# Four graph layers on one core: the first layer's relation made row by row and turned by transposes, its norm from ScalarE's squares, its centring on GpSimd

## The chip, the cores and the metric

The kernel runs on 1 core of one Trainium2 chip. The metric is the device time of one execution in microseconds, the median of several runs. All times below are microseconds unless marked ns.

## The reference

There are 64 graphs of 128 nodes with 256 features each, and one adjacency matrix `adj` (128 x 128, zeros and ones) for all. Four layers follow each other, each of the form x = x + layer(relu(layernorm(x))). The change touches the first:

```python
def _L0_gnn_ref(neuron_states, adjacency, Wq, Wk, Wv):
    q = jnp.einsum('bnd,ed->bne', neuron_states, Wq)
    k = jnp.einsum('bnd,ed->bne', neuron_states, Wk)
    v = jnp.einsum('bnd,ed->bne', neuron_states, Wv)
    rel = jnp.einsum('bnd,bmd->bnm', q, k)
    rel = adjacency.T[None, :, :] * rel
    rel = rel / jnp.linalg.norm(rel, axis=2, keepdims=True)
    return jnp.einsum('bnm,bmd->bnd', rel, v)
...
h = jnp.maximum(_layernorm(x, axis=-1), 0.0)
x = x + _L0_gnn_ref(h, adj, L0_gnn_Wq, L0_gnn_Wk, L0_gnn_Wv)
```

The other three are an attention with a leaky ReLU, a product with the normalised adjacency, and an attention with 8 heads.

## The kernel before

All of x stays in SBUF (`xs`). The graphs are worked on in 32 pairs, and each layer goes through all pairs before the next begins. Each engine has its own instruction stream, written by hand, and semaphores tie the streams together; so the order in which a function stands in an engine's `step` is the order in which that engine does it. In the first layer `step(p)` is run for p = 1 to 30 on TensorE (PE), with what comes before pair 1 and after pair 30 written out around it.

For pair p the work of the first layer is, in the order of its data:

- VectorE (DVE) takes the mean and variance of both graphs (`statistics`, lines 115 to 130: two BN_STATS, two BN_AGGR, then `nmean` and `vare`), GpSimd (POOL) raises the variance to the power -1/2 (`inverse_root`, line 141), and DVE's `normalise` (line 526) writes the centred features `xn`.
- PE turns them by four transposes into bank `HT` (`turn`, line 152). ScalarE (ACT) makes the rounded part of their ReLU (`relu_high`, line 390), DVE the remainder (`low_part`, line 569), and ACT once more the full one, `hT` (`relu_T`, line 395). A product of rounded and remainder parts takes 3 matmuls where one of full precision stood.
- PE multiplies by the joint weight of q and k (`t_product`, 12 matmuls, line 246), and ACT copies the result (`copy_t`, line 399). PE multiplies by the weight of v (`values`, 12 matmuls, line 246); ACT makes the rounded part (`copy_v`, line 404) and DVE the remainder (`low_v`, line 581).
- PE makes the relation matrix (`relation`, line 308) in bank `RR`, with the receiving node along the free dimension, and DVE multiplies it by `adj` (`mask`, line 576, tile `relm`). ACT makes its rounded part (`relation_high`, line 409), GpSimd its remainder (`relation_low`, line 468) and its squares (`squares`, line 464).
- In `outputs(p)` PE first sums the squares over the partitions by products with a column of ones (line 316, bank `NO`), and then multiplies the relation by the values (6 matmuls, line 321, bank `OO`). DVE copies the sums (`copy_norm2`, line 586), GpSimd raises them to -1/2 (`inverse_norm`, line 473), and DVE adds the scaled result to x (`update`, line 591).

PE's `step(p)` is `t_product(p)`, `turn(p+1)`, `values(p)`, `relation(p)`, `outputs(p-1)`. There is one `hT`, one pair `hTs` of rounded part and remainder, and one `relm`; so `relu_high(p+1)` waits until `values(p)` has read `hTs`. The second layer's first product (line 236) waits for the last `update` of the first layer. During steps 1 to 6 ACT and DVE also split the later layers' weights (lines 413 and 565).

## Time and profile before

| | before |
|---|---|
| median of 3 runs | 769.87 (768.22 to 770.98) |
| the profiled execution: its time | 770.85 |
| the profiled execution: its span, first to last instruction | 769.1 |
| busy: PE, PEld, DVE, ACT, POOL | 722.0, 668.5, 648.3, 551.6, 485.8 |
| mean granted TensorE clock, share of full | 0.984 |

PE is TensorE's matmuls, PEld its weight loads, which run beside them: each matmul has one load, and a matmul on full-precision operands that are not turned shows as two or more of each. The span is that of one profiled execution, and what lies around it is the difference of the first two of its numbers. The first layer takes the stretch from the start to 191.6; the rest of the span belongs to layers that the change does not touch.

### The profile page before, as it was taken

What the parts mean: (1) busy time and instruction counts of PE and PEld (TensorE: products, weight loads), DVE (VectorE), ACT (ScalarE), POOL (GpSimd) and SP (SyncE); (2) the same over time, 40 slices, a digit from 0 to 9 for tenths busy, and PEclk for the clock granted to TensorE, in tenths of its full rate; (3) what the DMA queues carried; (4) which work ended last, traced back from release to release, by engine and by line L of the source; (5) the groups of instructions that cost most, each with busy time, mean ns of one, the idle gap of its engine ahead of it and who ended that gap; (6) DMA issues with size and microseconds to landing.
All of it is one profiled execution on the core that took longest, in us unless ns stands there. A gap on an engine that the chain in (4) does not pass through costs nothing.

```text
span 769.1 us, 23106 instructions
## 1 busy us (share of the span) xinstructions
PE 722.0 (94%) x7001; PEld 668.5 (87%) x7001; DVE 648.3 (84%) x2709; ACT 551.6 (72%) x1768; POOL 485.8 (63%) x615
## 2 busy tenths in 40 slices
PE   6999999997999989869999899999999999999995
PEld 5999999997777777769998799999999999999984
DVE  5898888887699999969998788888888888888863
ACT  3554545443578778756663899999999999999985
POOL 1445455456477877668884667666667666667652
PEclk9999999999999999979999999999999999999999
DMA  7333200000000000000000000000000000000001
GB/s 231 96 97 96 68 0 0 0 0 1 1 1 1 2 1 1 1 1 0 0 0 1 2 29 29 14 28 28 27 28 28 14 28 28 27 28 28 14 29 42
DMA packets 21681, 20.15 MB, mean 26 GB/s; under 512 B 2432, under 2 KB 21632, under 8 KB 21632
## 3 DMA queue, kind: packets, MB, share of 16 engines
q1 hardware_dynamic: 19440, 18.16, 7.4%
q10 hardware_dynamic: 2192, 1.44, 0.7%
q8 instruction: 17, 0.28, 0.1%
q14 instruction: 32, 0.26, 0.1%
HBM read 11.21 MB, written 8.39 MB: 25 GB/s over the span
## 4 chain that ended last, share of the span: by engine, by line
PE 76%; DVE 16%; issue 3%; ACT 1%; POOL 1%; DMA 1%; DVEq 0%; POOLq 0%; ACTq 0%
PE bank L246 42%; PE bank L1072 7%; PE bank L1064 5%; PE bank L1082 4%; PE bank L152 4%; PE bank L308 4%; PE bank L321 3%; PE bank L226 3%; DVE stats L115 3%; DVE xs L843 2%; DVE masked_e L819 2%; DVE leaky_e L824 2%; PE bank L236 2%; PE bank L316 2%; DVE att L837 1%
## 5 line engine op out<-in xcount | busy, mean ns | idle before, releaser
L1141 ACT ACTIVATE prob<-wide,small 128x128 f32<-128x128 f32 x512 | 199.1, 395 | 20.1 <-DVE small L1225 20.0
L1190 POOL TENSOR_TENSOR prob<-prob,small 128x512 f32<-128x512 f32 x128 | 133.1, 1040 | 106.1 <-DVE small L1239 106.1
L141 POOL TENSOR_TENSOR rstd<-vare,mhalf 128x2 f32<-128x2 f32 x128 | 88.6, 692 | 67.8 <-DVE vare L130 67.8
L1225 DVE CUSTOM_DVE_ANT_0 wide<-bank,mbias 128x128 f32<-128x128 f32 x512 | 116.0, 282 | 9.4 <-PE bank L1064 9.4
L115 DVE BATCH_NORM_STATS2 stats<-xs 128x6 f32<-128x256 f32 (+1 forms) x256 | 95.4, 414 | 5.6 <-DMA xs<-in_x_dram 4.5
L1141 ACT ACTIVATION_READ_ACCUMULATOR prob<-wide,small 128x1 f32 x512 | 98.2, 192 | 0.0
L217 POOL TENSOR_SCALAR xn<-xs,nmean,rstd 128x256 f32<-128x256 f32 x126 | 69.1, 558 | 13.6 <-POOL rstd L141 10.8
L1148 ACT COPY probT<-bank 128x512 f32<-128x512 f32 x128 | 72.0, 588 | 7.8 <-PE bank L1072 6.9
L1072 PE MATMUL bank<-ident,prob 128*128 128x128 f32 x512 | 73.8, 276 | 1.9 <-POOL prob L1190 1.7
L236 PE MATMUL bank<-w,hT 128*128 128x258 f32 x256 | 63.0, 389 | 2.3 <-DVE xs L591 1.9
L1072 PEld LDWEIGHTS bank<-ident,prob 128*128 128x128 f32 x512 | 57.1, 140 | 8.9 <-issue 6.0
L246 PE MATMUL bank<-w,yTs 128*128 128x256 f32 x384 | 55.4, 295 | 4.5 <-DVE xs L968 4.5
L152 PE MATMUL bank<-ident,xn 128*128 128x128 f32 x384 | 58.4, 275 | 0.5 <-DVE xn L1000 0.5
L236 PEld LDWEIGHTS bank<-w,hT 128*128 128x128 f32 x256 | 49.3, 194 | 10.6 <-DVE xs L591 2.2
L464 POOL TENSOR_TENSOR relsq<-relm 128x256 f32<-128x256 f32 x32 | 21.6, 676 | 56.0 <-PE bank L321 56.0
L246 PE MATMUL bank<-wo,oTs 128*128 128x256 f32 x384 | 54.8, 293 | 2.2 <-DVE oTs L1248 2.2
L246 PE MATMUL bank<-hTs,wq 128*128 128x256 f32 x384 | 55.0, 293 | 1.8 <-DVE hTs L1243 1.8
L246 PEld LDWEIGHTS bank<-w,yTs 128*128 128x128 f32 x384 | 49.5, 196 | 6.4 <-DVE yTs L963 4.7
L246 PE MATMUL bank<-wv0T,hTs 128*128 128x256 f32 x384 | 54.0, 289 | 0.7 <-DVE oTs L581 0.7
L246 PEld LDWEIGHTS bank<-wo,oTs 128*128 128x128 f32 x384 | 48.1, 192 | 6.3 <-DVE oTs L1248 2.7
L246 PE MATMUL bank<-wv,hTs 128*128 128x256 f32 x384 | 53.0, 287 | 0.0
L246 PE MATMUL bank<-hTs,m_qk 128*128 128x256 f32 x384 | 50.9, 281 | 0.8 <-DVE hTs L569 0.8
(128 smaller groups left out, 1843.8 us busy)
## 6 DMA issues: line engine op xcount, KB each, us to landing
out_dram<-xs SPq DMA_DIRECT2D x32, 256.0 KB, 2.1
xs<-in_x_dram SPq DMA_DIRECT2D x29, 256.0 KB, 2.6
xs<-in_x_dram ACTq DMA_DIRECT2D x1, 512.0 KB, 7.3
xs<-in_x_dram ACTq DMA_DIRECT2D x1, 256.0 KB, 3.8
wq<-in_L_gnn_Wq_dram SPq DMA_DIRECT2D x1, 256.0 KB, 3.4
wk<-in_L_gnn_Wk_dram ACTq DMA_DIRECT2D x1, 256.0 KB, 4.7
wv<-in_L_gnn_Wv_dram SPq DMA_DIRECT2D x1, 256.0 KB, 5.3
w<-in_L_gnn_W_dram SPq DMA_DIRECT2D x1, 256.0 KB, 7.1
```

The lines of the kernel that those rows point to most:

```text
L115: ins = nc.vector.bn_stats(stats[:, b, g, :], x_of(p, g))
L141: nc.gpsimd.tensor_tensor(rstd[:, b, :], vare[:, b, :], mhalf[:, :], ALU.pow).then_inc(rstd_ready, 1)
L152: ins = nc.tensor.transpose(pe_ps[:, c * 2 * N + g * N:c * 2 * N + (g + 1) * N], src[:, g, c * 128:(c + 1) * 128], ident[:, :])
L217: ins = nc.gpsimd.tensor_scalar(xnb[b][:, g, :], xs[:, 2 * p + g, :], nmean[:, b, g:g + 1], rstd[:, b, g:g + 1], ALU.add, ALU.mult)
L236: ins = nc.tensor.matmul(ps_g, hT[:, c, g, :], weight[:, c, :], start=(c == 0), stop=(c == C - 1))
L246: ins = nc.tensor.matmul(ps, lhsT(a, c), rhs(b, c), start=(n == 0), stop=(n == len(terms) - 1))
L1064: ins = nc.tensor.matmul(SS[r][:, (g * C + c) * N:(g * C + c + 1) * N], qT[rows_r, c, g, :], kT[rows_r, c, g, :], start=True, stop=True)
L1072: ins = nc.tensor.transpose(PT[r % 2][:, i * N:(i + 1) * N], prob[:, r, i, :], ident[:, :])
L1141: ins = nc.scalar.activation(prob[:, r, i, :], wide[:, r, i, :], ACT.Exp, bias=nmax[r][:, i:i + 1], scale=-1.0, accum_out=rsum[r][:, i:i + 1])
L1148: nc.scalar.copy(probT[:, r, :, :].rearrange("p i n -> p (i n)"), PT[r % 2][:, :]).then_inc(pt_ready, 1)
L1190: nc.gpsimd.tensor_tensor(prob[:, r, :, :], prob[:, r, :, :], rinv[r].unsqueeze(2).to_broadcast([128, QUAD, N]), ALU.mult).then_inc(prob_r ...
L1225: nc.vector.tensor_tensor_reduce(out=wide[:, r, i, :], in0=SS[r][:, i * N:(i + 1) * N], in1=mbias[:, :], scale=-1.0, scalar=3e38, op0=ALU. ...
```

## The change

Six things change in the first layer.

1. `relation` swaps its operands, so the relation has the receiving node along the partitions; `mask` multiplies it by a transposed adjacency `adjT`, made once at the start by one PE transpose and one DVE copy, and writes to one of two `relm`. PE turns the masked relation by two transposes into bank `RT` (`turn_relation`), and `relation_high` and `relation_low` read `RT`.
2. The squares and their sums are made by two ACT instructions, one for each graph, which square a row and sum it (`squares`); PE's product with ones, `copy_norm2` and the bank `NO` are gone.
3. `relation_low` moves from GpSimd to DVE, where it reads PSUM.
4. Centring moves from DVE to GpSimd (`centre`, two instructions for a pair), but for the first two pairs.
5. `hT` gets a second buffer `hT2`, and `hTs` a second one in `yTs[0]`, which the third layer uses later; so `relu_high(p+1)` no longer waits for `values(p)`.
6. The order of each engine's step is written anew, the work on the masked relation of pair p-1 now being done in step p, and `update` stands ahead of `low_v`.

```diff
+        hTs_of = [hTs, yTs[0]]
+        hT_of = [hT, hT2]
...
-                ins = nc.gpsimd.tensor_scalar(xnb[b][:, g, :], xs[:, 2 * p + g, :], nmean[:, b, g:g + 1],
+                ins = nc.gpsimd.tensor_scalar(xnb[b][:, g, :], x_of(p, g), nmean[:, b, g:g + 1],
...
+                def turn_relation(p, b):
+                    pe.wait_ge(relm_ready, p + 1)
+                    pe.wait_ge(relm_low, since(p))
+                    for g in range(2):
+                        ins = nc.tensor.transpose(RT[:, g * N:(g + 1) * N], relm[b][:, g, :], ident[:, :])
+                    ins.then_inc(rt_done, 1)
...
+                def relation(p, b):
                     pe.wait_ge(tT_ready, p + 1)
                     pe.wait_ge(hT_ready, p + 1)
                     pe.wait_ge(relm_ready, since(p))
                     for g in range(2):
                         for c in range(C):
-                            ins = nc.tensor.matmul(RR[:, g * N:(g + 1) * N], hT[:, c, g, :], tT[:, c, g, :],
+                            ins = nc.tensor.matmul(RR[:, g * N:(g + 1) * N], tT[:, c, g, :], hT_of[b][:, c, g, :],
                                                    start=(c == 0), stop=(c == C - 1))
                     ins.then_inc(rel_done, 1)
 
                 def outputs(p):
-                    pe.wait_ge(relsq_ready, p + 1)
                     pe.wait_ge(x_done, since(p))
-                    for g in range(2):
-                        nc.tensor.matmul(NO[:, g:g + 1], relsq[:, g, :], ones[:, 0:1], start=True, stop=True)
...
+                def step(p, b):
+                    t_product(p, b)
+                    turn(p + 1, 1 - b)
+                    turn_relation(p - 1, 1 - b)
+                    values(p, b)
+                    relation(p, b)
                     outputs(p - 1)
...
-                def relu_high(p):
+                def relu_high(p, b):
                     act.wait_ge(tr_done, p + 1)
-                    act.wait_ge(v_done, since(p))
-                    nc.scalar.activation(hT_high, HT[:, :], ACT.Relu).then_inc(high_ready, 1)
-
-                def relu_T(p):
+                    act.wait_ge(v_done, since(p - 1))
+                    nc.scalar.activation(flat(hTs_of[b][0]), HT[:, :], ACT.Relu).then_inc(high_ready, 1)
+
+                def relu_T(p, b):
                     act.wait_ge(low_ready, p + 1)
-                    act.wait_ge(rel_done, since(p))
-                    nc.scalar.activation(hT_flat, HT[:, :], ACT.Relu).then_inc(hT_ready, 1)
+                    act.wait_ge(rel_done, since(p - 1))
+                    nc.scalar.activation(flat(hT_of[b]), HT[:, :], ACT.Relu).then_inc(hT_ready, 1)
...
                 def relation_high(p):
+                    act.wait_ge(rt_done, p + 1)
+                    act.wait_ge(out_done, since(p))
+                    nc.scalar.copy(rels[0][:, :, :], RT[:, 0:2 * N].rearrange("p (g n) -> p g n", g=2)).then_inc(relm_high, 1)
+
+                def squares(p, b):
                     act.wait_ge(relm_ready, p + 1)
-                    act.wait_ge(out_done, since(p))
-                    nc.scalar.copy(rels[0][:, :, :], relm[:, :, :]).then_inc(relm_high, 1)
+                    act.wait_ge(rn_ready, since(p))
+                    for g in range(2):
+                        ins = nc.scalar.activation(relsq[:, g, :], relm[b][:, g, :], ACT.Square, accum_out=norm2[:, g:g + 1])
+                    ins.then_inc(n2_ready, 1)
...
+
+                def step(p, b):
                     copy_t(p)
-                    relu_high(p + 1)
-                    relu_T(p + 1)
+                    relu_high(p + 1, 1 - b)
+                    relation_high(p - 1)
+                    squares(p - 1, 1 - b)
+                    relu_T(p + 1, 1 - b)
                     copy_v(p)
-                    relation_high(p)
...
-                def squares(p):
-                    pool.wait_ge(relm_ready, p + 1)
-                    pool.wait_ge(out_done, since(p))
-                    nc.gpsimd.tensor_tensor(relsq[:, :, :], relm[:, :, :], relm[:, :, :], ALU.mult).then_inc(relsq_ready, 1)
-
-                def relation_low(p):
-                    pool.wait_ge(relm_high, p + 1)
-                    nc.gpsimd.tensor_tensor(rels[1][:, :, :], relm[:, :, :], rels[0][:, :, :].bitcast(F32),
-                                            ALU.subtract).then_inc(relm_low, 1)
-
                 def inverse_norm(p):
                     pool.wait_ge(n2_ready, p + 1)
+                    pool.wait_ge(x_done, since(p))
                     nc.gpsimd.tensor_tensor(rnorm[:, :], norm2[:, :], mhalf[:, :], ALU.pow).then_inc(rn_ready, 1)
...
+                pool.wait_ge(tr_done, 1)
+                centre(pool, 2, 0, rstd_ready, xn_ready)
+
+                def step(p, b):
+                    inverse_root(pool, p + 2, stats_ready, rstd_ready, b)
                     inverse_norm(p - 1)
-                    relation_low(p)
-                    inverse_root(pool, p + 3, stats_ready, rstd_ready)
-
-                with pool.Fori(0, PAIRS // 2 - 2) as j:
-                    step(2 * j + 1)
-                    step(2 * j + 2)
-                for n, p in enumerate(range(PAIRS - 3, PAIRS)):
-                    squares(p)
-                    inverse_norm(p - 1)
-                    relation_low(p)
-                    if n > 0:
-                        inverse_root(pool, n - 1, l1_stats_ready, l1_rstd_ready, (n - 1) % 2)
-                        if n == 1:
-                            pool.wait_ge(tr_done, PAIRS)
-                        centre(pool, n - 1, (n - 1) % 2, l1_rstd_ready, l1_xn_ready)
+                    pool.wait_ge(tr_done, p + 1)
+                    centre(pool, p + 2, b, rstd_ready, xn_ready)
+
+                for p in range(1, PAIRS - 2):
+                    step(p, p % 2)
...
+                def mask(p, b):
                     dve.wait_ge(rel_done, p + 1)
-                    dve.wait_ge(relsq_ready, since(p))
-                    dve.wait_ge(relm_low, since(p))
-                    nc.vector.tensor_tensor(relm[:, :, :], RR[:, 0:2 * N].rearrange("p (g n) -> p g n", g=2),
-                                            adj_pair, ALU.mult).then_inc(relm_ready, 1)
+                    dve.wait_ge(rt_done, since(p - 1))
+                    dve.wait_ge(n2_ready, since(p - 1))
+                    nc.vector.tensor_tensor(relm[b][:, :, :], RR[:, 0:2 * N].rearrange("p (g n) -> p g n", g=2),
+                                            adjT_pair, ALU.mult).then_inc(relm_ready, 1)
+
+                def relation_low(p):
+                    dve.wait_ge(relm_high, p + 1)
+                    nc.vector.tensor_tensor(rels[1][:, :, :], RT[:, 0:2 * N].rearrange("p (g n) -> p g n", g=2),
+                                            rels[0][:, :, :].bitcast(F32), ALU.subtract).then_inc(relm_low, 1)
 
...
-                def copy_norm2(p):
-                    dve.wait_ge(out_done, p + 1)
-                    nc.vector.tensor_copy(norm2[:, :], NO[:, 0:2]).then_inc(n2_ready, 1)
-
                 def update(p):
                     dve.wait_ge(rn_ready, p + 1)
+                    dve.wait_ge(out_done, p + 1)
...
-                def step(p):
-                    low_part(p + 1)
-                    mask(p)
-                    normalise(p + 2)
+                def step(p, b):
+                    low_part(p + 1, 1 - b)
+                    relation_low(p - 1)
+                    dve.wait_ge(xn_ready, p + 2)
+                    statistics(p + 3, 1 - b)
+                    mask(p, b)
+                    update(p - 1)
                     low_v(p)
-                    copy_norm2(p - 1)
-                    statistics(p + 3)
-                    update(p - 1)
```

TensorE's stream, a whole step before (`t_product`, `turn`, `values`, `relation`, the sums, the outputs; bank is PSUM):

```order
L246 MATMUL bank<-hTs,m_qk 128x256 x12
L152 MATMUL bank<-ident,xn 128x128 x4
L246 MATMUL bank<-wv0T,hTs 128x256 x12
L308 MATMUL bank<-tT,hT 128x128 x4
L316 MATMUL bank<-ones,relsq 128x1 x2
L321 MATMUL bank<-oTs,rels 128x256 x6
```

The same step in the changed kernel:

```order
L253 MATMUL bank<-hTs,m_qk 128x256 x12
L153 MATMUL bank<-ident,xn 128x128 x4
L304 MATMUL bank<-ident,relm 128x128 x2
L253 MATMUL bank<-wv0T,hTs 128x256 x12
L323 MATMUL bank<-hT,tT 128x128 x4
L333 MATMUL bank<-oTs,rels 128x256 x6
```

The two products with `ones` (which the trace shows as four) are gone, and two transposes of `relm` stand ahead of the 12 products for the values.

VectorE's stream before, from the `update` that ends one step (with a weight's remainder behind it, in this early step) through the next one up to its statistics:

```order
L591 SCALAR_TENSOR_TENSOR xs<-bank,rnorm,xs 128x256 x2
L565 TENSOR_TENSOR wv_1<-raw,wv_0 128x512
L569 SCALAR_TENSOR_TENSOR hTs<-bank,hTs 128x512
L576 TENSOR_TENSOR relm<-bank,adj_sb 128x256
L526 TENSOR_SCALAR xn<-xs,mv,rstd 128x256 x2
L581 TENSOR_TENSOR oTs<-bank,oTs 128x512
L586 COPY norm<-bank 128x2
L115 BN_STATS stats<-xs 128x6 x2
L122 BN_AGGR mv<-stats 128x2 x2
L129 SCALAR_TENSOR_TENSOR nmean<-mv 128x2
L130 SCALAR_TENSOR_TENSOR vare<-mv 128x2
```

The same in the changed kernel, one step, from `low_part` (here into the second buffer, `yTs`) to `low_v`:

```order
L578 SCALAR_TENSOR_TENSOR yTs<-bank,yTs 128x512
L590 TENSOR_TENSOR rels<-bank,rels 128x256
L116 BN_STATS stats<-xs 128x6 x2
L123 BN_AGGR mv<-stats 128x2 x2
L130 SCALAR_TENSOR_TENSOR nmean<-mv 128x2
L131 SCALAR_TENSOR_TENSOR vare<-mv 128x2
L585 TENSOR_TENSOR relm<-bank,adjT 128x256
L602 SCALAR_TENSOR_TENSOR xs<-bank,rnorm,xs 128x256 x2
L595 TENSOR_TENSOR oTs<-bank,oTs 128x512
```

Centring (`xn`) and the copy of `norm` have left; `rels` has come; the mask stands behind the statistics; and `low_v` (`oTs`), which stood ahead of the statistics, is last, behind `update` (`xs`).

GpSimd's stream before, one step of its loop:

```order
L464 TENSOR_TENSOR relsq<-relm 128x256
L473 TENSOR_TENSOR rnorm<-norm,mhalf 128x2
L468 TENSOR_TENSOR rels<-relm,rels 128x256
L140 REGISTER_ALU
L141 TENSOR_TENSOR rstd<-vare,mhalf 128x2
```

GpSimd's stream in the changed kernel, two steps:

```order
L142 TENSOR_TENSOR rstd<-vare,mhalf 128x2
L490 TENSOR_TENSOR rnorm<-norm,mhalf 128x2
L224 TENSOR_SCALAR xn<-xs,nmean,rstd 128x256 x2
L142 TENSOR_TENSOR rstd<-vare,mhalf 128x2
L490 TENSOR_TENSOR rnorm<-norm,mhalf 128x2
L224 TENSOR_SCALAR xn<-xs,nmean,rstd 128x256 x2
```

The two large two-input operations on the relation (`relsq` and `rels`) have left, and the two centring operations have come, behind the power for the norm.

## Rows read from the trace of the kernel before

**Rows 1.** windows of the steady first layer and its end: us, then busy us of each engine, PEclk

```profile
99.89:174.76 74.87, 74.87 (x647) 74.87 (x645) 64.73 (x197) 37.41 (x71) 38.78 (x56) 1.00 0.00 0
174.76:191.60 16.84, 12.83 (x106) 12.12 (x104) 11.54 (x39) 5.81 (x12) 10.88 (x18) 0.93 0.00 1
```

**Rows 2.** timeline of one step: start us, us, engine, line, operation [idle before <-releaser]

```profile
99.89 1.48 PEld L246 LDWEIGHTS bank<-hTs,m_qk 128*128 128x128 f32 x12
...
101.31 0.46 PEld L152 LDWEIGHTS bank<-ident,xn 128*128 128x128 f32 x4
...
101.50 0.74 DVE L115 BATCH_NORM_STATS2 stats<-xs 128x6 f32 x2
101.61 0.58 ACT L399 COPY tT<-bank 128x512 f32<-128x512 f32 x1 [0.52 <-PE bank L246]
...
101.74 1.50 PEld L246 LDWEIGHTS bank<-wv0T,hTs 128*128 128x128 f32 x12
...
102.31 0.73 POOL L468 TENSOR_TENSOR rels<-relm,rels 128x256 fp32r<-128x256 f32 x1
...
102.63 0.43 DVE L129 SCALAR_TENSOR_TENSOR nmean<-mv 128x2 f32<-128x2 f32 x1
...
103.05 0.86 DVE L591 SCALAR_TENSOR_TENSOR xs<-bank,rnorm,xs 128x256 f32 x2
103.18 0.98 PEld L308 LDWEIGHTS bank<-tT,hT 128*128 128x128 f32 x8
...
103.56 0.60 ACT L390 ACTIVATE hTs<-bank 128x512 fp32r<-128x512 f32 x1 [1.36 <-PE bank L246]
104.08 0.53 PEld L316 LDWEIGHTS bank<-ones,relsq 128*128 128x128 f32 x4
104.19 0.69 DVE L569 SCALAR_TENSOR_TENSOR hTs<-bank,hTs 128x512 fp32r<-128x512 f32 x1 [0.27 <-ACT hTs L390]
...
104.52 0.78 PEld L321 LDWEIGHTS bank<-oTs,rels 128*128 128x128 f32 x6
...
104.79 0.41 DVE L576 TENSOR_TENSOR relm<-bank,adj_sb 128x256 f32<-128x256 f32 x1
...
105.23 1.48 PEld L246 LDWEIGHTS bank<-hTs,m_qk 128*128 128x128 f32 x12
```

**Rows 3.** timeline, TensorE's weight loads, start of the program

```profile
17.18 1.47 PEld L246 LDWEIGHTS bank<-hTs,m_qk 128*128 128x128 f32 x12 [0.45 <-issue]
...
19.97 1.49 PEld L246 LDWEIGHTS bank<-wv0T,hTs 128*128 128x128 f32 x12 [0.92 <-DVE oTs L581]
```

**Rows 4.** timeline, end of the first layer and first product of the second

```profile
180.11 1.48 PEld L246 LDWEIGHTS bank<-hTs,m_qk 128*128 128x128 f32 x12
...
180.43 0.16 DVE L586 COPY norm<-bank 128x2 f32<-128x2 f32 x1 [0.34 <-PE bank L321]
...
187.04 0.88 DVE L591 SCALAR_TENSOR_TENSOR xs<-bank,rnorm,xs 128x256 f32<-128x256 f32 x2
...
190.66 0.88 DVE L591 SCALAR_TENSOR_TENSOR xs<-bank,rnorm,xs 128x256 f32<-128x256 f32 x2 [0.81 <-POOL rnorm L473]
...
191.59 3.81 PE L236 MATMUL bank<-w,hT 128*128 128x258 f32 x8 [1.93 <-DVE xs L591]
```

**Rows 5.** timeline, VectorE and GpSimd, near the end of the first layer

```profile
177.43 0.16 DVE L129 SCALAR_TENSOR_TENSOR nmean<-mv 128x2 f32<-128x2 f32 x1
...
188.45 1.09 POOL L217 TENSOR_SCALAR xn<-xs,nmean,rstd 128x256 f32<-128x256 f32 x2
...
188.97 0.20 DVE L129 SCALAR_TENSOR_TENSOR nmean<-mv 128x2 f32<-128x2 f32 x1
```

**Rows 6.** the page's costliest groups: busy us, mean ns of one

```profile
L1141 ACT ACTIVATE prob<-wide,small 128x128 f32<-128x128 f32 x512 | 199.1, 395 | 20.1 <-DVE small L1225 20.0
...
L141 POOL TENSOR_TENSOR rstd<-vare,mhalf 128x2 f32<-128x2 f32 x128 | 88.6, 692 | 67.8 <-DVE vare L130 67.8
...
L217 POOL TENSOR_SCALAR xn<-xs,nmean,rstd 128x256 f32<-128x256 f32 x126 | 69.1, 558 | 13.6 <-POOL rstd L141 10.8
```

154 lines of the change are left out of this document (77 added, 77 removed).

## The prediction, on record before the changed kernel ran

> **What bounds the kernel now.** I read the stretches first. From 99.89 to 174.76 TensorE is busy 74.87 of 74.87 us, its weight loads too, at full clock, while VectorE has 64.73, ScalarE 37.41 and GpSimd 38.78 [rows 1]. That stretch holds 14 steps, so a step takes 5.348. Next the timeline of one step [rows 2]. The weight loads of each group start when the group before them has issued, so the differences of their starts are what each group costs TensorE: `t_product` 1.42 (99.89 to 101.31), four transposes 0.43, `values` 1.44, `relation` 0.90, sums of squares 0.44 (104.08 to 104.52), outputs 0.71, together 5.34. None of these rows has idle time before it. So the middle of the first layer costs TensorE's issue time, and only what leaves or enters TensorE's stream counts there, as long as the others keep pace. The exceptions are at its two ends. At the start TensorE waits 0.45 for pair 1's remainder and 0.92 for pair 0's values [rows 3]. At the end, from the start of `t_product(31)` at 180.11 to the second layer's first product at 191.59 pass 11.48 us, in which TensorE waits for `update(30)` (187.04) and `update(31)` (190.66), and both stood behind sums, copy and power [rows 4].
>
> **The change, part by part.**
>
> *TensorE, each step.* The sums leave: 0.44. Two transposes come. Four transposes take 0.43, so two take 0.215 [rows 2]; the swap in `relation` leaves its four products of the same size. The step becomes 5.34 - 0.44 + 0.215 = 5.115, a gain of 0.225. From below the two transposes can't be less than nothing (gain 0.44); from above I take what the two sum products took, 0.44 (gain 0). I take 0.215, since it is the same operation on the same shape.
>
> *Does VectorE keep pace?* I lay a step out from t = 0 at the start of `t_product(p)`. ScalarE's `copy_t` starts at 1.72 (101.61) [rows 2] and takes 0.58, `relu_high(p+1)` 0.60 behind it, so to 2.90. (The turn has issued by 1.85, and its buffer is free, so this no longer waits for `values(p)`, as it did at 103.56.) VectorE then runs `low_part` from 2.93 (start to start with the mask 0.60 [rows 2]), `relation_low` (new: 128 x 256 from PSUM with an SBUF operand, as the mask, 0.41), the statistics, the mask 0.41, `update` and `low_v`. The statistics took 1.55 (101.50 to 103.05), of which `nmean` 0.43. The same `nmean` took 0.16 at 177.43 [rows 5]; at 102.63 it ended at 103.06, just when GpSimd's `rels` of 102.31 ended (103.04) [rows 2]. GpSimd no longer does that operation, so I take 1.28. The mask then ends at 2.93 + 0.60 + 0.41 + 1.28 + 0.41 = 5.63. `update(p-1)` needs the outputs, whose end VectorE sees 0.32 behind the next `t_product` (180.43 against 180.11 [rows 4]), at 5.44; so it starts at 5.63, takes 0.86 [rows 2], and `low_v` 0.69 (the same size and form as `low_part`) ends at 7.18, which is 2.07 in the next step. `values(p+1)` wants it at 1.42 + 0.43 + 0.215 = 2.065. So with every duration counted in full the fit is exact to 0.01, with no slack; but instructions that follow each other without a wait overlap by about 0.08 (0.60 against 0.69 [rows 2]), five times in this chain, on ScalarE too, and then `update` is bound by the outputs at 5.44 and `low_v` ends about 1.85, 0.2 early. I take no wait. This is the narrowest place of the design.
>
> *The relation's way.* Two transposes end about 2.35, `relation_high` follows `relu_high` (2.90 to at most 3.50, its bound being the 128 x 512 ReLU), `relation_low` ends at 3.94, and the outputs want it at 1.42 + 0.43 + 0.215 + 1.44 + 0.90 = 4.405. No wait. The squares are 2 ScalarE instructions with sums, not in this layer before; the fourth layer's exponentials of 128 x 128 with sums take 395 ns each [rows 6], so 0.79, and I allow 0.2 for reading out the last sum: 3.50 to 4.5. ScalarE then has some 1.0 more a step, against 37.41 of 74.87 busy [rows 1]; it is hidden under TensorE. If it were not, it would cost 30 steps of it.
>
> *GpSimd.* Squares and remainder leave, two centrings come, 558 ns each [rows 6]. Its chain is the squares' end 4.5, the power 0.69 (692 ns for the same 128 x 2 form), centring 1.12, so 6.35 with a step between engines, which is 1.23 in the next step, and `turn` wants it at 1.42. With ScalarE's overlaps it is some 0.3 earlier. Hidden. The power for the norm is ready at about 5.2, before `update`.
>
> *The start.* The two waits of rows 3 go: `relu_high(1)` need not wait for `values(0)`, and VectorE no longer centres pair 2 ahead of `mask(0)` and `low_v(0)`. One transpose for `adjT` costs 0.11. Gain 0.45 + 0.92 - 0.11 = 1.26, at least 0.
>
> *The end.* From `t_product(31)` = 0: `turn_relation(30)` to 1.64; `values(31)` waits for `low_v(30)` to about 1.9; `relation` from 3.3; outputs(30) 4.2 to 4.95; `update(30)` at 5.27, since its power is long made, to 6.15; `low_v(31)` to 6.85, `relation_low(31)` to 7.25, outputs(31) from 7.3 to 8.0, seen at 8.35; `update(31)` 8.4 to 9.3, for its power too is made beside that; the second layer's product at 9.35. Before it was 11.48 [rows 4]: gain 2.1. Bounds: 0, and 3.
>
> *Sum.* 30 steps of 0.225 = 6.75, start 1.26, end 2.1: 10.1. From the profiled execution's 770.85 that is 760.7, and since that execution was 0.98 above the median, **759.8** as a median.
>
> **The port.** While GpSimd centres (188.45, two instructions, 1.09), `nmean` inside that time took 0.20, not 0.16 [rows 5]; so centring costs VectorE's two-input operations a few hundredths. The Trainium skill (Advanced Engine Details and Errata, GPSIMD Details) says more: that GpSimd shares a read and a write interface with VectorE and conflicts with VectorE instructions that have two SBUF inputs. `nmean` is one, and in the changed order it lies where GpSimd centres. The row at 102.63 agrees, the row at 188.97 hardly does; what it would cost if it held is the second rival.
>
> **The rivals.**
>
> 1. *VectorE is late after all* (chance 0.12). For it: the chain above has no slack with full durations, and `low_v` now stands last. A step would be about as long as before, 5.3 to 5.35; only the ends gain, 3.4: 766.5. Against it: VectorE loses the centring of 2 x 256 elements, the copy (0.16 [rows 4]) and 0.27 of stretched `nmean`, and gains one operation of 0.41.
> 2. *Centring holds VectorE's `nmean`* to its end: up to 1.1, and by where the two fall in my layout about 0.7. `low_v` ends at 2.55 instead of 1.85, so `values` starts 0.5 late. The long step then gives VectorE the time back, so the wait comes in every second step: 30 x 0.25 = 7.5 lost, 767.3. Against it the 0.20 above. Chance 0.06.
> 3. *Two transposes cost what the sums did*, and the change does nothing for TensorE in the steps: ends only, 766.5. Chance 0.05.
> 4. *Slower: the ring through GpSimd.* Turn, `relu_high`, `relation_high`, squares, power, centring, next turn is one ring, 0.2 to 0.5 short of a step. It decides when it grows by more than that; to end 0.3% above the median of before it must make the step 0.19 longer than 5.34, so grow by some 0.6 to 0.9, as it would if power and centring each took half as long again (0.35 + 0.55 = 0.9). At 0.9, with 0.35 of slack, a step is 5.115 + 0.55 = 5.665: 30 x 0.325 = 9.75 lost, 3.4 gained at the ends, 776.2. For it: GpSimd's durations beside new traffic are unknown; against: 558 ns is a mean over 126 [rows 6]. Chance 0.04.
>
> *The clock at the end* goes with each case. It fell to half there: 8 products took 3.81 at 191.59 behind an idle stretch of 1.93 [rows 4], and TensorE was busy 12.83 of the 16.84 us that end there, at a mean clock of 0.93 [rows 1]. In my layout the 2.1 us that go are all idle time of TensorE. If the clock stays up, half of 3.81 comes back, 1.9, giving 757.9; I give it 4 in 10, within the forecast's case.
>
> **How the numbers follow.** Forecast 0.73, split into 759.8 and 757.9; rivals 0.12, 0.06, 0.05, 0.04. A measurement of this kernel tells about 0.3% (2.3 us) from no change. The range from 756.5 to 767.5 takes in the forecast with the clock's case, up to 1.4 more if the 0.44 bound is nearer, and rivals 1 to 3 nearly whole. Faster: the forecast and rivals 1 to 3 all end under 767.56, but rivals 1 to 3 lie near it, so of their 0.23 I count 0.06 as no change: 0.90. Slower: 0.04.
>
> **What would show it.** The step, from one `t_product` to the next, at 5.10 to 5.15 (right), at 5.3 (rival 1 or 2; then `values` loads show idle time before them, released by VectorE's `oTs`), or transposes of `relm` with a group cost of 0.44 (rival 3). `nmean` at 0.16 to 0.20 (right) or 0.5 and more (rival 2). Idle time ahead of `turn`'s transposes, released by GpSimd's `xn` (rival 4). The first `t_product`s without 0.45 and 0.92 of idle time. The end, `t_product(31)` to the second layer's product, at about 9.4. ScalarE's two squares of a pair within about 1.0. The prediction is wrong if a step is over 5.2 or if the later layers, which the change leaves alone, get longer.

## The result: 755.25 us, 1.8% faster, and outside the predicted range

| | before | after |
|---|---|---|
| median | 769.99 (768.22 to 770.98), 4 runs | 755.25 (754.75 to 756.56), 4 runs |
| ratio after to before | | 0.9818, 95% interval 0.9803 to 0.9833 |
| the profiled execution: time, span | 770.85, 769.1 | 755.72, 753.8 |
| mean granted clock | 0.984 | 0.989 |

The prediction was 759.8, range 756.5 to 767.5. The direction was right, but the change brought 14.7 us and not 10.1. The median lies 1.25 us below the range.

The middle of the first layer first. These are the windows of the kernel after, from the start of one `t_product` to that of `t_product(31)`, and from there to the second layer's first product; the columns are those of [rows 1].

```profile
94.86:171.46 76.60, 76.60 (x663) 76.60 (x661) 59.30 (x176) 45.75 (x135) 36.35 (x61) 1.00 0.01 4
171.46:180.75 9.29, 6.83 (x55) 6.18 (x53) 7.20 (x25) 3.98 (x14) 4.36 (x8) 1.00 0.01 2
```

TensorE and its weight loads are still busy the whole time, as in [rows 1], and 15 steps take 76.60, so a step takes 5.107 where it took 5.348. VectorE has gone from 86% to 77% of the stretch, ScalarE from 50% to 60%. One step in the timeline (start, duration, engine, line, operation), which answers to [rows 2]:

```profile
94.86 1.48 PEld L253 LDWEIGHTS bank<-hTs,m_qk 128*128 128x128 f32 x12
...
96.17 0.68 DVE L595 TENSOR_TENSOR oTs<-bank,oTs 128x512 fp32r<-128x512 f32 x1
96.28 0.46 PEld L153 LDWEIGHTS bank<-ident,xn 128*128 128x128 f32 x4
...
96.71 0.25 PEld L304 LDWEIGHTS bank<-ident,relm 128*128 128x128 f32 x2
...
96.93 1.49 PEld L253 LDWEIGHTS bank<-wv0T,hTs 128*128 128x128 f32 x12
...
97.81 0.33 ACT L431 ACTIVATE relsq<-relm 128x128 f32<-128x128 f32 x1
...
98.31 0.21 ACT L431 ACTIVATION_READ_ACCUMULATOR relsq<-relm 128x1 f32 x1
```

The reader is to see two things. The two transposes of `relm` cost TensorE 0.22 (96.71 to 96.93), as half of four transposes did. And no weight load has idle time before it.

Where VectorE's `nmean` meets GpSimd's centring matters further down, so here are the two kinds of meeting that this kernel shows, with the two centring instructions of a pair taken singly:

```profile
58.79 0.56 POOL L224 TENSOR_SCALAR xn<-xs,nmean,rstd 128x256 f32<-128x256 f32 x1
58.96 0.39 DVE L130 SCALAR_TENSOR_TENSOR nmean<-mv 128x2 f32<-128x2 f32 x1 [0.26 <-DVE mv L123]
...
99.28 0.56 POOL L224 TENSOR_SCALAR xn<-xs,nmean,rstd 128x256 f32<-128x256 f32 x1
...
99.78 0.16 DVE L130 SCALAR_TENSOR_TENSOR nmean<-mv 128x2 f32<-128x2 f32 x1
...
99.82 0.56 POOL L224 TENSOR_SCALAR xn<-xs,nmean,rstd 128x256 f32<-128x256 f32 x1
```

At 58.96 `nmean` began 0.17 into a centring instruction, took 0.39 and ended with it at 59.35. At 99.78 it began 0.06 before the end of the first and 0.04 before the start of the second, and took 0.16. Of the 28 meetings in this profile, 27 are of the second kind.

The end of the first layer, which answers to [rows 4]:

```profile
171.46 1.48 PEld L253 LDWEIGHTS bank<-yTs,m_qk 128*128 128x128 f32 x12
...
173.38 1.49 PEld L253 LDWEIGHTS bank<-wv0T,yTs 128*128 128x128 f32 x12 [0.26 <-DVE oTs L595]
...
178.73 0.77 PEld L333 LDWEIGHTS bank<-oTs,rels 128*128 128x128 f32 x6 [1.60 <-issue]
...
179.82 0.88 DVE L602 SCALAR_TENSOR_TENSOR xs<-bank,rnorm,xs 128x256 f32<-128x256 f32 x2
...
180.75 3.07 PE L243 MATMUL bank<-w,hT 128*128 128x258 f32 x8 [1.05 <-DVE xs L602]
```

From `t_product(31)` to the second layer's first product pass 9.29 us (11.48 before). That product takes 3.07 (3.81 before, 2.01 at full clock when the kernel was run again), since part of it still ran at half clock.

Laid side by side, the two profiled executions differ by 15.3 us of span, and the table says where. Each row is the difference of two starts of TensorE's weight loads, or of a start and the end of the span.

| stretch | before | after | gained |
|---|---|---|---|
| start to `t_product(1)` | 17.18 | 17.03 | 0.15 |
| `t_product(1)` to `t_product(31)` | 162.93 | 154.43 | 8.50 |
| `t_product(31)` to the second layer's first product | 11.48 | 9.29 | 2.19 |
| second layer, from its first product to the third layer's | 138.8 | 136.3 | 2.5 |
| third layer | 85.95 | 86.7 | -0.75 |
| fourth layer | 352.8 | 350.1 | 2.7 |

The first three rows make 10.84, beside a predicted 10.1. The other 4.5 came in code that the change doesn't touch. What is different there is seen in two places. The first is the granted clock (PEclk) in windows of the kernel before, and then of the kernel after:

```profile
189.00:196.00 7.00, 5.07 (x16) 3.75 (x15) 2.42 (x11) 0.57 (x1) 3.66 (x7) 0.51 0.00 1
329.00:336.00 7.00, 5.92 (x24) 5.56 (x25) 4.66 (x13) 4.75 (x10) 3.38 (x4) 0.51 0.01 2
...
424.00:428.00 4.00, 3.32 (x15) 3.32 (x16) 2.72 (x21) 4.00 (x21) 1.96 (x3) 0.58 0.00 0
762.00:766.00 4.00, 2.93 (x12) 2.63 (x12) 0.98 (x2) 0.00 (x0) 0.00 (x0) 0.57 0.00 0
```

```profile
181.00:184.00 3.00, 3.00 (x10) 2.33 (x10) 0.87 (x6) 0.14 (x1) 1.62 (x3) 0.59 0.00 0
314.00:321.00 7.00, 4.23 (x17) 4.05 (x18) 4.41 (x14) 5.43 (x13) 2.80 (x4) 0.55 0.00 1
...
424.00:428.00 4.00, 4.00 (x59) 3.66 (x58) 2.81 (x17) 4.00 (x20) 2.36 (x3) 1.00 0.00 0
745.00:752.00 7.00, 3.22 (x48) 2.51 (x47) 1.38 (x2) 1.17 (x2) 0.00 (x0) 1.00 0.13 40
```

The clock has two levels here, 1.2 and 2.4 GHz, and 0.50 is the lower. Before fell to it in five places (a fifth is at 342 to 347), after in three (a third is at 328 to 336), and not in the fourth layer. The second is the second layer's steps. A step here is the time from one pair's first product (`w`, `hT`) to the next pair's. From the 8th on nearly all take 4.04, and those ahead of it 3.2 to 4.0, but for the first with 5.25 before and 4.61 after. Before had one of 5.07 (the 7th, 215.34 to 220.41) and one of 5.14 (the 20th), after had none. The start of the long one in the kernel before:

```profile
214.12 1.27 POOL L797 TENSOR_TENSOR xs<-xs,exp_u 128x512 f32<-128x512 f32 x1
...
214.34 1.33 DVE L824 SCALAR_TENSOR_TENSOR leaky_e<-masked_e 128x256 f32<-128x256 f32 x1
...
215.34 1.71 PEld L236 LDWEIGHTS bank<-w,hT 128*128 128x128 f32 x8
...
218.19 0.20 PEld L686 LDWEIGHTS bank<-ident,att 128*128 128x128 f32 x2 [1.13 <-DVE att L837]
...
219.28 0.43 DVE L824 SCALAR_TENSOR_TENSOR leaky_e<-masked_e 128x256 f32<-128x256 f32 x1
...
219.41 1.44 POOL L797 TENSOR_TENSOR xs<-xs,exp_u 128x512 f32<-128x512 f32 x1
...
220.41 1.72 PEld L236 LDWEIGHTS bank<-w,hT 128*128 128x128 f32 x8
```

`leaky_e` is a VectorE operation with both inputs in SBUF. It began at 214.34 inside GpSimd's add of 214.12 to 215.39, and ended at 215.67, 0.28 behind it, having taken 1.33 where it takes 0.43. One step later it began 0.13 ahead of the add, took its 0.43, and the add took 1.44 in place of 1.27. The `leaky_e` of the other long step began at 267.93, only 0.02 ahead of the add of 267.95, and took 1.57; it too ended 0.28 behind the add's end. So a `leaky_e` that begins inside the add, or as good as together with it, ends 0.28 behind the add, while one that begins 0.13 ahead of it loses nothing. The transposes of `att` then waited until 218.19. In the profiled execution of after, the order was the harmless one, here at 202.93, in every step but the last two of the layer, in which `leaky_e` took 0.68 in both kernels:

```profile
202.93 0.44 DVE L835 SCALAR_TENSOR_TENSOR leaky_e<-masked_e 128x256 f32<-128x256 f32 x1
...
203.06 1.44 POOL L808 TENSOR_TENSOR xs<-xs,exp_u 128x512 f32<-128x512 f32 x1
```

The Trainium skill (Advanced Engine Details and Errata, GPSIMD Details) says that GpSimd shares an interface with VectorE and conflicts with VectorE instructions that have two SBUF inputs. By that rule this is the place to look, and these rows agree, with 0.90 lost for one collision. So does the row at 58.96 in the first layer, where `nmean` has two SBUF inputs.

### The profile page after: what moved, and what is told of

Read it like the earlier page. It is cut to its first block, busy times and chain, and to the rows that moved or that the text cites. A ratio compares the mean times of both kernels' runs of the same rounds, so it can differ in the third digit from the quotient of the medians.

```text
span 753.8 us, 22983 instructions
## 1 busy us (share of the span) xinstructions
PE 709.9 (94%) x6938; PEld 657.7 (87%) x6938; DVE 627.1 (83%) x2650; ACT 564.8 (75%) x1896; POOL 474.5 (63%) x610
## 3 DMA queue, kind: packets, MB, share of 16 engines
q10 hardware_dynamic: 2192, 1.44, 0.7%
## 4 chain that ended last, share of the span: by engine, by line
PE 76%; DVE 16%; issue 4%; ACT 1%; POOL 1%; DMA 1%; DVEq 0%; POOLq 0%; ACTq 0%
PE bank L253 43%; PE bank L1083 7%; PE bank L1075 5%; PE bank L1093 4%; PE bank L323 4%; PE bank L153 4%; PE bank L233 3%; PE bank L333 3%; DVE stats L116 3%; DVE xs L854 2%; DVE masked_e L830 2%; DVE leaky_e L835 2%; DVE att L848 2%; DVE small L838 2%; PE bank L243 1%
## 5 line engine op out<-in xcount | busy, mean ns | idle before, releaser
L224 POOL TENSOR_SCALAR xn<-xs,nmean,rstd 128x256 f32<-128x256 f32 x186 | 102.4, 561 | 12.8 <-POOL rstd L142 10.8
L490 POOL TENSOR_TENSOR rnorm<-norm,mhalf 128x2 f32<-128x2 f32 x32 | 22.1, 691 | 79.9 <-ACT relsq L431 79.9
L253 PE MATMUL bank<-hTs,wk 128*128 128x256 f32 x384 | 51.2, 282 | 0.0
L253 PEld LDWEIGHTS bank<-hTs,wq 128*128 128x128 f32 x384 | 47.9, 189 | 2.3 <-DVE hTs L1254 2.3
```

Source lines behind the costliest of these rows:

```text
L224: ins = nc.gpsimd.tensor_scalar(xnb[b][:, g, :], x_of(p, g), nmean[:, b, g:g + 1], rstd[:, b, g:g + 1], ALU.add, ALU.mult)
L253: ins = nc.tensor.matmul(ps, lhsT(a, c), rhs(b, c), start=(n == 0), stop=(n == len(terms) - 1))
```

## The experiments

My theory was that the 4.5 us behind the first layer come from two things that code left alone can still meet: collisions of `leaky_e` with GpSimd's add, and falls of the clock. The rivals were that they are chance of one execution, so that the change is worth its 10.8 alone, or that they hang on something else that the first layer leaves behind. The theory as written also said that the collisions move when the later layers begin some tenths of a microsecond earlier or later. Beside this, the terms of the first layer were put to a test. There are twelve runs. Where no count of rounds is named, a run is one execution, set beside the kernel before on the same chip (one execution, and seven with a median of 770.14 for the last four kernels). The kernel before alone spread from 768.22 to 770.98, so differences of 1 to 2 us are read from stretches of the profiles and not from whole times.

**Both kernels again.** No edit.

> The kernel before, once more, for the stretch that the change does not touch: from the second layer's first product to the end (769.1 - 191.6 = 577.5 us in the profiled execution of before; 753.8 - 180.75 = 573.0 in that of the changed kernel, 4.5 less with the same code). Theory A (coincidences: two-input operations of VectorE and GpSimd that meet, and where TensorE's clock falls, both hanging on phases of some tenths of a us): the stretch comes out between 574 and 579, possibly again 577.5 if the phases repeat. Theory B (something lasting that the changed first layer leaves behind): 577.5 within 0.5.

> The changed kernel, once more, same stretch. Theory A: between 571 and 576, 573.0 if the phases repeat. Theory B: 573.0 within 0.5. Both: step of the first layer 5.107, end of the first layer 9.29.

Measured: 768.99 and 754.05, the kernel before beside them 770.64. Behind the second layer's first product, 574.9 and 571.1 us of span were left, 3.8 apart (the first pair 4.5). The two long steps of the second layer came back in the kernel before at the same places (4.94 and 5.18), `leaky_e` again at 1.33 in the first:

```profile
214.91 1.27 POOL L797 TENSOR_TENSOR xs<-xs,exp_u 128x512 f32<-128x512 f32 x1
...
215.13 1.33 DVE L824 SCALAR_TENSOR_TENSOR leaky_e<-masked_e 128x256 f32<-128x256 f32 x1
```

The third layer's falls of the clock came back in both kernels. The fourth layer's did not: both took 350.1. So the 2.7 us of the fourth layer were chance of one execution, and the rest was not. In return the fall at the start of the second layer, which after had shown, was absent now. So a difference of nearly the same size came back, but made of other terms: 3.1 in the second layer (2.5 in the first pair), 0.8 in the third (-0.75) and nothing in the fourth (2.7). The two stretches fit the theory's ranges (574 to 579, 571 to 576) and lie outside those of its rival. The new order had one collision in this run, in the 6th step of 5.08, with `leaky_e` at 197.38 inside the add of 197.22 and 1.40 long. And in the kernel before the clock fell earlier than in the first pair, at 187.4 and not at 189.1, so that the end of the first layer took 12.36 and not 11.48.

**Both kernels, shifted by half a microsecond.**

```diff
+                for _ in range(5):
+                    nc.tensor.transpose(bank[7][:, 0:128], ident[:, :], ident[:, :])
                 with pe.Fori(3, PAIRS // 2 - 1) as j:
```

> Before with 5 more transposes of the identity on TensorE behind step 6 of the first layer (0.54 us at 0.108 each; their result is not used). Nothing but the moment at which the later layers begin is shifted. Theory A: the stretch behind the second layer's first product changes by 1 us or more, either way, and the two places in the second layer where a step takes 5.07 and 5.14 in place of 4.04 move or vanish. Theory B: it stays 577.5 within 0.5.

> The changed kernel with the same 5 transposes (0.54 us, result not used). Theory A: the stretch behind the second layer's first product changes by 1 us or more from 573.0, most likely upward. Theory B: it stays 573.0 within 0.5.

Measured: 770.03 and 754.3. In the old kernel the second layer began at 192.68, 0.41 later than in the repeated run (192.27) and 1.09 later than in the first (191.59). Yet the long steps stood in the same places in all three, the 7th and the 20th of the layer, and 575.5 was left behind its first product, against 574.9. So a shift by tenths doesn't move the collisions; that part of the theory fell, and the rival's 577.5 within 0.5 did not come either. In the changed kernel the edit says little, since the program's start came earlier by about as much and the layer began at 180.83 (180.89 when repeated); one long step was the 6th in both, and 571.6 was left against 571.1, so the move upward that was most expected did not come. Two of the kernels further down say more for the new order, though they were made for other things: `a_extra2` enters the second layer at 187.03 and `a_one_buffer` at 223.35, 6 and 42 us later, and in both the 6th step is again the long one, at 5.08 and 5.09. In the first run of after, whose first two products lie 4.61 apart and not 3.19, the 6th took 4.00. So the layer's own rhythm from its first product on leads to a collision or past it, and not the time at which the layer begins, as far as these runs go; nothing was run to change that rhythm alone.

**The collision taken out of the kernel before.** GpSimd's add of the second layer waits until VectorE's `leaky_e` of the same step is done.

```diff
+                        pool.wait_ge(leaky_ready, p)
                         add(p - 4)
```

> Before, with one wait added in the second layer: GpSimd's add of a pair begins only once VectorE's leaky_e of that step is done, so the two two-input operations can't start in the order in which VectorE then waits for GpSimd. Theory A (collisions: VectorE's leaky_e stood 0.9 to 1.0 us behind GpSimd's add in two steps of 32): no step of the second layer takes 4.9 to 5.2 any more and that layer takes about 2.0 less than 138.8. Theory B (the long steps come from elsewhere, or GpSimd's delay is itself the bound): the layer takes as long as before or longer.

Measured: 766.27, beside 768.7 for the kernel before: 2.4 us less. The second layer took 135.9 and not 138.8. The group of `leaky_e` before, and here (busy us, then mean ns of one):

```profile
L824 DVE SCALAR_TENSOR_TENSOR leaky_e<-masked_e 128x256 f32<-128x256 f32 x32 | 16.4, 512 | 1.1
```

```profile
L825 DVE SCALAR_TENSOR_TENSOR leaky_e<-masked_e 128x256 f32<-128x256 f32 x32 | 14.0, 438 | 1.1
```

The two long steps, the 7th and the 20th, took 4.03 each, which is 2.1 of the layer's 2.9. Another 0.45 is the first product's gap, 4.80 where it had been 5.25, which is the clock's. As only the order of the two instructions was changed, this shows the collision as the cause of the long steps, with its size. It agrees with the theory's 2.0 less.

**TensorE kept busy where the clock falls, with products and with transposes.** The results of the added products go to a bank that nothing reads.

```diff
+                for _ in range(5):
+                    nc.tensor.matmul(bank[7][:, 0:128], ident[:, :], ident[:, :], start=True, stop=True)
                 outputs(PAIRS - 1)
+                for _ in range(4):
+                    nc.tensor.matmul(bank[7][:, 0:128], ident[:, :], ident[:, :], start=True, stop=True)
...
+                pe.wait_ge(leaky_ready, PAIRS)
+                for _ in range(12):
+                    nc.tensor.matmul(bank[4][:, 0:128], ident[:, :], ident[:, :], start=True, stop=True)
...
+                    if p == 2:
+                        for _ in range(14):
+                            nc.tensor.matmul(bank[4][:, 0:128], ident[:, :], ident[:, :], start=True, stop=True)
```

The first two stand at the end of the first layer, the third at that of the second, the fourth in the third layer's start. The other kernel has transposes in their place, twice as many.

> The changed kernel with filler on TensorE where it stood idle between layers: 5 and 4 products of the identity with itself at the end of the first layer, 12 at the end of the second, 14 in the third's beginning, each in a stretch in which TensorE waited anyway; their results are not used. Theory A (the fall of TensorE's clock after these idle stretches is what the later layers lose or gain between executions): granted clock 1.00 throughout, first product of the second layer 3.2 before the second one, third layer below 84.5 in place of 85.2 to 86.7; about 2 us off the whole. Theory B (the clock costs nothing there, since TensorE isn't what is waited for): clock up, time the same.

> The same with transposes of the identity in place of the products, two for each, so for the same time. By theory A the time follows the granted clock, whichever it is. Two sub-theories on what keeps the clock: any TensorE work (then as a_keep), or products alone (then the clock falls as without filler, and the time is that of the changed kernel).

Measured: 752.68 and 754.08. Windows around the start of the third layer and the two places in the fourth, first of the unedited kernel after (run again), then with products, then with transposes:

```profile
311.00:336.00 25.00, 17.32 (x104) 16.18 (x105) 18.27 (x55) 13.67 (x30) 16.77 (x22) 0.80 0.00 1
404.00:412.00 8.00, 5.81 (x71) 5.42 (x70) 6.57 (x38) 3.54 (x16) 4.35 (x7) 1.00 0.00 0
```

```profile
311.00:336.00 25.00, 22.40 (x177) 21.11 (x178) 20.75 (x64) 15.30 (x33) 18.80 (x25) 1.00 0.01 2
404.00:412.00 8.00, 5.83 (x60) 5.43 (x59) 5.81 (x34) 5.33 (x25) 2.83 (x4) 0.79 0.01 2
```

```profile
311.00:336.00 25.00, 22.31 (x177) 20.91 (x178) 20.76 (x64) 15.35 (x32) 18.77 (x25) 1.00 0.01 2
404.00:412.00 8.00, 5.82 (x60) 5.42 (x58) 5.76 (x34) 5.33 (x25) 2.82 (x4) 0.79 0.01 2
740.00:750.00 10.00, 5.93 (x60) 4.89 (x58) 2.25 (x4) 2.63 (x7) 1.04 (x1) 0.83 0.08 26
```

In 311 to 336 the clock stays at 1.00 with either filler, where it was 0.80, and the third layer takes 82.9 rather than 85.2. But in both kernels a fall came in the fourth layer at 407, which the unedited kernel hadn't shown, and in the second one more at 745. The fourth layer took 350.1, 351.4 and 352.7 with none, one and two falls. So each of these falls cost 1.3, and filling one gap doesn't stop the next. The theory had 1.00 throughout and 2 us off the whole; the third layer gave 2.4, and the fall at 407 took 1.3 of it back. Transposes served here as products did. At the border ahead of the second layer these two runs say nothing, for the unedited repeat had no fall there either.

**Centring back on VectorE.** GpSimd's `centre(p + 2)` leaves its step.

```diff
+                def centre_dve(p, b):
+                    dve.wait_ge(rstd_ready, p + 1)
+                    dve.wait_ge(tr_done, p - 1)
+                    for g in range(2):
+                        ins = nc.vector.tensor_scalar(xnb[b][:, g, :], x_of(p, g), nmean[:, b, g:g + 1],
+                                                      rstd[:, b, g:g + 1], ALU.add, ALU.mult)
+                    ins.then_inc(xn_ready, 1)
...
                     relation_low(p - 1)
+                    centre_dve(p + 2, b)
```

> The changed kernel with centring of pairs 3 to 31 of the first layer given back to VectorE, ahead of the statistics. VectorE's chain from low_part to low_v grows by 0.7, and low_v was 0.2 early. By the prediction's timetable values waits by turns, a step takes 5.3 to 5.35 in place of 5.107, and the kernel 6 to 7 us more. Rival (VectorE has 0.9 us of idle time in a step, which takes it up): 5.107, no change.

Measured: 761.59, 7.5 more than the repeated kernel after; 2.6 of that is two falls of the clock in the fourth layer, and 4.7 is the first layer. Steps alternate between 5.10 (141.85 to 146.95) and 5.51 (146.95 to 152.46):

```profile
141.85 1.49 PEld L253 LDWEIGHTS bank<-wv0T,hTs 128*128 128x128 f32 x12 [0.37 <-DVE oTs L593]
...
146.95 1.49 PEld L253 LDWEIGHTS bank<-wv0T,yTs 128*128 128x128 f32 x12
...
152.46 1.50 PEld L253 LDWEIGHTS bank<-wv0T,hTs 128*128 128x128 f32 x12 [0.37 <-DVE oTs L593]
```

The steps are to be read from one `values` to the next. Every second time it waits 0.37 for `low_v`, and the long step gives VectorE the time back. A little more on VectorE makes it the bound, as the predicted absence of slack said, so moving centring to GpSimd is worth 0.20 a step. Over the thirty steps that made 5.6, for this run's `t_product(1)` came 0.9 earlier than the repeated run's; the 6 to 7 that were expected are met only together with the clock's falls.

**One buffer for the split features and one for the features.**

```diff
-        hTs_of = [hTs, yTs[0]]
-        hT_of = [hT, hT2]
+        hTs_of = [hTs, hTs]
+        hT_of = [hT, hT]
...
-                    act.wait_ge(v_done, since(p - 1))
+                    act.wait_ge(v_done, since(p))
...
-                    act.wait_ge(rel_done, since(p - 1))
+                    act.wait_ge(rel_done, since(p))
```

> The changed kernel with one buffer each for hT and for hTs, so relu_high(p+1) waits for values(p) and relu_T(p+1) for relation(p) as in before; all else as changed. By the prediction's timetable relu_high goes from 2.2 to 3.8 us behind the step's start, VectorE's chain behind it ends at 8.5, and the ring values, relu_high, low_part, statistics, mask, update, low_v, values takes 6.5: a step 6.5 in place of 5.107, some 795 in all. Rival (the buffers don't matter, TensorE's issue is the bound): 5.107.

Measured: 796.49, beside a median of 770.14 for the kernel before. A step takes 6.55 (103.26 to 109.81):

```profile
102.59 0.94 PE L333 MATMUL bank<-oTs,rels 128*128 128x256 f32 x6 [1.00 <-DVE rels L590]
...
103.26 1.48 PEld L253 LDWEIGHTS bank<-hTs,m_qk 128*128 128x128 f32 x12
...
107.34 0.60 ACT L406 ACTIVATE hTs<-bank 128x512 fp32r<-128x512 f32 x1 [1.77 <-PE bank L253]
...
109.81 0.78 PEld L253 LDWEIGHTS bank<-hTs,m_qk 128*128 128x128 f32 x6
```

`relu_high` waits 1.8 for `values`, `relation_high` stands behind it on ScalarE, and TensorE's outputs wait 1.0 for the remainder of the relation. So the new order of work rests on the second buffers. Without them the change would be 26 us slower than before.

**Two more transposes in each step.**

```diff
                 def turn_relation(p, b):
...
+                    for _ in range(2):
+                        nc.tensor.transpose(RT[:, 256:384], ident[:, :], ident[:, :])
```

> The changed kernel with two more transposes of the identity in each turn_relation of the first layer (result not used), 0.215 of TensorE's issue. Theory (issue-bound step): 5.107 + 0.215 = 5.32, so about 6.7 us more. Rival (the step is set by the ring through VectorE, whose slack was reckoned at 0.2 us): less than 5.25, or the two together, over 5.35.

Measured: 760.57, and 5.325 a step, 0.218 more than 5.107, where 0.215 was expected. What TensorE issues is what a step costs, to a hundredth, up to there.

**All the clock's gaps filled and the collision gone, in both kernels**, each in 3 rounds. Beside the edits of the two kernels above, six products stand behind the fourth layer's first scores and five ahead of its last output product.

```diff
+                    if isinstance(p, int) and p == 0:
+                        for _ in range(6):
+                            nc.tensor.matmul(bank[5][:, 0:128], ident[:, :], ident[:, :], start=True, stop=True)
...
+                            for _ in range(5):
+                                nc.tensor.matmul(bank[3][:, 0:128], ident[:, :], ident[:, :], start=True, stop=True)
```

> The changed kernel with filler products at the three places of a_keep, 6 more behind the fourth layer's first scores and 5 ahead of its last output product (results not used), and with the wait of b_guard in the second layer. If clock and collisions are all that varies behind the first layer: granted clock 1.00 throughout, second layer 134.8, third 82.9, fourth 350.1, so about 568 us behind the second layer's first product, and 750.3 in all. If the filler gets in the way of the work: the fourth layer over 350.5.

> The kernel before with the same filler and wait. Theory A (what the change gained behind the first layer was clock and collisions alone): the stretch behind the second layer's first product is as long as in a_best, within 0.7; the whole is longer than a_best by what the first layer alone gained, 10.8 to 11.2. Theory B (something of the first layer lasts): the stretch is 2 us or more longer than in a_best.

Measured: the changed kernel with them 750.16 (750.1 to 750.76), ratio to before 0.9744 (0.9728 to 0.976); the kernel before with them 761.04 (760.55 to 761.55), ratio 0.9881 (0.9864 to 0.9897). Windows of the former:

```profile
171.00:186.00 15.00, 14.24 (x101) 12.61 (x101) 10.76 (x36) 5.09 (x17) 7.62 (x13) 1.00 0.00 1
310.00:336.00 26.00, 23.71 (x188) 22.51 (x189) 21.73 (x69) 16.43 (x34) 19.91 (x26) 1.00 0.01 2
...
740.00:748.00 8.00, 4.06 (x54) 3.47 (x54) 1.38 (x2) 0.98 (x2) 0.00 (x0) 1.00 0.20 67
```

The first product of the second layer takes 2.01 now, and no fall is left in its profile, whose layers came within 0.4 us of what was expected. This pair answers the question of the 4.5 us: with the collisions and nearly every fall out of both, the two kernels differ by 10.88 as medians. Their second layers begin at 180.73 and 191.47, 10.74 apart. Behind it 567.4 and 568.3 are left. Those 0.9 are a little over the 0.7 that the theory allowed, and 0.8 of them lies in the fourth layer, where the second kernel has a fall of the clock at 747. So the change's own work is worth 10.8, nearly all in the first layer. The further 3.9 us of the medians (14.74 less 10.88) came from clock and collisions. Filler and guard alone brought 5.1 us on the changed kernel and 9.0 on the one before, beside the 10.9 of the change itself.

## Why the prediction was right, and where it failed

**Right: TensorE's issue is the bound.** Two transposes were taken at 0.215 and measured 0.22; adding two more cost 0.218 each step. The rival that they cost what the sums did is out.

**Right, and a little too small: the step's gain.** 5.348 less 5.107 is 0.24, beside a predicted 0.225, some 0.5 us over 30 steps. The 8.50 are made of 30 times 0.241 = 7.2, of the 0.92 of the start's second wait, which falls in the first of these steps, and of an item that I had not looked for: in four early steps, in which later weights are split, the kernel before took 5.47 to 5.49, and after 5.11, so another 0.5. One step of 5.28 (58.93 to 64.21) takes back 0.2; it is the one with the long `nmean`, of which more below.

**Right: VectorE, just.** `low_v` was to end 0.2 early. It ended at 96.85 (96.17 and 0.68), and `values` began at 96.93, so it was 0.08 early. Centring on VectorE uses up this slack and more.

**Right in the time, wrong in the reason: centring and `nmean`.** The prediction let centring cost a few hundredths, from the 0.20 of [rows 5], and gave rival 2, that centring holds `nmean`, a chance of 0.06. That row joins two instructions: taken singly they are 188.45 to 189.00 and 188.99 to 189.54, and `nmean` at 188.97 began 0.03 before the first one ended. So it was no test of an `nmean` inside a centring. The changed kernel has such a test at 58.96, and there rival 2's mechanism acts: `nmean` took 0.39 and ended with the centring instruction. The seven other profiles of the new order in which GpSimd centres show it once each, 0.37 to 0.39 long and ended within 0.01 of the centring's end. The cost follows the slack. The step was 0.17 longer in six of these eight profiles, not longer in `a_extra2`, whose steps give VectorE 0.2 more, and 0.38 longer in `a_one_buffer` (6.93 for 6.55), where VectorE is in the ring that sets the step. That it came in one step and not in thirty is because `nmean` began about 0.05 before the end of the first centring instruction in the other 27. The layout of the prediction had not worked that out, so that rival 2's 7.5 us stayed away was luck in part. And the prediction looked for the conflict only at the new instructions, while the larger one was in the second layer, in code that stayed.

**Right: the ring through GpSimd and the squares.** The two squares with their sums took 0.71 on ScalarE (97.81 to 98.52), within the 1.0 allowed. Centring ended at 100.38, 1.0 ahead of the transposes that read it.

**Right: the start.** Predicted 1.26. The two waits did go: no idle time stands ahead of the loads at 17.03 and 19.11.

```profile
12.29 1.48 PEld L253 LDWEIGHTS bank<-hTs,m_qk 128*128 128x128 f32 x12 [1.15 <-DVE hTs L578]
...
17.03 1.49 PEld L253 LDWEIGHTS bank<-yTs,m_qk 128*128 128x128 f32 x12
...
19.11 1.50 PEld L253 LDWEIGHTS bank<-wv0T,yTs 128*128 128x128 f32 x12
```

From `t_product(0)` to `t_product(1)` pass 4.74, where it was 5.09: 0.35 less, for a predicted 0.34 (0.45 less 0.11). The 0.92 came in full, in the first step (5.24 for 6.39). Together that is 1.27. In the profiled pair 0.20 of it was hidden, for `t_product(0)` itself started at 12.29, where it had been 12.09. But that start wanders with either kernel: it lay between 11.85 and 12.15 in the five profiles of the old order and between 11.53 and 12.45 in the nine of the new, so a difference of 0.20 between two executions is no effect of the change.

**Right: the end.** 2.19, predicted 2.1, through the steps as laid out. In the new order it took 9.29 or 9.30 in all nine profiles. In the old order it took 11.48, 12.36, 12.26 and 11.95 without filler and 11.29 with it, so the clock added 0.2 to 1.1 there, and this pair caught the least.

**Wrong: the sum had no term behind the first layer.** "The later layers, which the change leaves alone" were taken at their old length, and the clock was counted only for the one product at the layer's border, at 1.9 with a chance of 4 in 10. As medians, the change brought 14.74 for a predicted 10.1, so 4.6 was missing: some 0.7 in the first layer and 3.9 behind it (14.74 less the 10.88 of the pair with filler and guard). Three things were missed there.
- The kernel before lost 2.1 us to two collisions in the second layer (5.07 and 5.14 for 4.04). The changed kernel had none in its first profile and one of about 1.1 in the repeat. `b_guard` shows the cause by taking it away.
- The fall at the border costs more than its first product. The gap between the first two products of the second layer is 5.25 to 5.35 before (4.80 in `b_guard`), 4.61 in the first run of after and 3.19 where the clock stays up. So the border could be worth 2.1 there (it was worth 0.64 in the profiled pair), and the gap was 3.19 in eight of the nine profiles of the new order, the first run of after being the ninth.
- The falls in the third and fourth layers change from run to run. In the profiled pair they gave 2.7 in the fourth layer by chance, and took 0.75 in the third.

The range failed with it. Its lower end was set by the first layer's terms, and the profile of before had in view a stretch of half clock in every later layer and two steps that were a microsecond too long. Either would have been a reason to put the lower end some 4 us further down.

**Open.** The clock at the layers' border fell in all four profiles of the old order without filler, and in one of six of the new. In the old order with filler it did not fall (`b_best`, one profile), where the filler had cut TensorE's two idle stretches ahead of the product from 2.0 and 1.9 us to 0.9 and 1.1. So idle time has a part in it. It is not the whole, since the idle stretch of 1.65 us in the fourth layer was there in both profiles of the kernel before, and the clock fell behind it only in one. What decides between the two isn't shown. Nor is it shown why the rhythm after a fall at the border collides at the 7th and 20th step in the old order and nowhere in the one case of the new, nor why centring on VectorE, which ends with the first layer, left a 6th step of 4.74 and a 26th of 4.36. Why `nmean` begins inside a centring instruction in just one step of the first layer is open too.

## What to carry to other kernels

When TensorE's weight loads follow each other without a gap, price a change by what it adds to and takes from that stream. Done so, the sum for the first layer came out 0.7 us short of 10.8. Before trusting "the rest stays as it is", list the steps of the untouched stages that are longer than their neighbours, and the stretches at half clock; what stands there is in play whenever the stage ahead of it changes. Such stretches are also cheap to remove: idle-time products for the clock and one semaphore wait against a collision brought the changed kernel from 755.25 to 750.16, and the old one from 769.99 to 761.04.

## What the hardware showed that I had not expected

- A VectorE operation of 0.43 with two SBUF inputs took 1.33 and 1.57 when it began inside a two-input GpSimd add of 1.27 or 0.02 ahead of it, and ended 0.28 behind the add both times. Begun 0.13 earlier than the add, it cost the add 0.17 instead.
- GpSimd's centring, with one SBUF tensor input, holds such a VectorE operation too, but only to the end of the instruction that runs: `nmean` of 0.16 took 0.39 when it began 0.17 into a centring of 0.56. A row that joins several instructions hides this.
- Transposes of a constant kept the granted clock at 1.00 in 311 to 336, as products did.
- A fall of the clock in the fourth layer cost 1.3 us each in four profiles (seven falls), and 0.8 in `b_best`, where the late one came 12 us ahead of the end and not 6.6. Taking away those near 330 was followed by one at 407 in both kernels in which that was all.
